# Rounding to fp8 once per tile in place of once per half: the VectorE queue of two attention passes

## What is computed

```python
def _div_clamp_fp8(x, scale):
    y = jnp.clip(x.astype(jnp.float32) / scale, -FP8_MAX, FP8_MAX)   # FP8_MAX = 448
    y = y.astype(jnp.bfloat16).astype(jnp.float32)
    return y.astype(jnp.float8_e4m3fn).astype(jnp.float32)

core = _gqa(q, k, v).reshape(b, s, nh * d)        # own keys and values
xout = _gqa(qx, kx, vx).reshape(b, s, nh * d)     # keys and values of the context
cat = jnp.concatenate([core, xout], axis=-1)
catq = _div_clamp_fp8(cat, proj_smooth)
return jnp.einsum('bsi,oi->bso', catq, wproj) * (proj_in_scale * proj_w_scale)
```

## Time and profile before

| | |
|---|---|
| time, median of 3 runs (lowest to highest) | 634.34 us (633.56 to 635.05) |
| the profiled execution: span from first to last instruction | 632.0 us |
| PE busy | 576.7 us, 91% |
| VectorE busy | 494.6 us, 78%, 924 instructions |
| ScalarE busy | 369.1 us, 58% |
| GpSimd busy | 365.9 us, 58% |
| mean granted TensorE clock | 0.986 |

### The profile page before, as it was taken

How to read it: one execution, slowest core, us unless ns; L and a number is a source line. 1 busy time by engine, 2 the same in 40 slices (tenths; PEclk the granted TensorE clock), 3 DMA queues, 4 the chain that set the end, 5 groups by cost and what they waited for, 6 DMA issues and landing times.

```text
span 632.0 us, 10614 instructions
## 1 busy us (share of the span) xinstructions
PE 576.7 (91%) x3735; PEld 468.2 (74%) x3738; DVE 494.6 (78%) x924; ACT 369.1 (58%) x669; POOL 365.9 (58%) x299
## 2 busy tenths in 40 slices
PE   3999679959869999999988999999999999999996
PEld 1664225635548888988977889888889888888886
DVE  4697999775999998999998889999997956333333
ACT  1559657757766776776766676667665235434221
POOL 4101495014578787868659967676777634855431
PEclk9999999988989999999998999999999999999999
DMA  7892113015512131031192141222210100310001
GB/s 219 272 348 77 60 50 117 34 67 152 180 33 106 35 111 58 1 134 35 48 357 96 37 124 57 86 84 85 59 43 18 35 0 3 117 37 30 1 2 67
DMA packets 44564, 54.87 MB, mean 87 GB/s; under 512 B 8416, under 2 KB 30816, under 8 KB 44512
## 3 DMA queue, kind: packets, MB, share of 16 engines
q1 hardware_dynamic: 44512, 54.20, 26.5%
HBM read 41.60 MB, written 12.58 MB: 86 GB/s over the span
## 4 chain that ended last, share of the span: by engine, by line
PE 64%; DVE 6%; POOL 3%; issue 3%; ACT 2%; DVEq 0%; POOLq 0%; ACTq 0%
PE g_proj L2217 13%; PE g_proj L2303 8%; PE g_scores L2258 7%; PE g_turn L2247 6%; PE g_op L2284 5%; PE g_op L474 3%; PE g_op L475 2%; PE g_op L476 2%; PE g_proj L459 2%; PE g_proj L461 2%; PE g_proj L460 2%; PE g_turn L2267 2%; PE g_op L2225 1%; POOL g_rs L1615 1%; PE g_turn L459 1%
## 5 line engine op out<-in xcount | busy, mean ns | idle before, releaser
L1615 POOL TENSOR_TENSOR g_rs<-g_ve,neg_half 128x4 f32<-128x4 f32 x80 | 83.7, 1052 | 36.4 <-DVE g_ve L1727 36.0
L1636 POOL TENSOR_TENSOR g_cat<-g_yb,g_kb 128x1024 fp32r<-128x1024 bf16 x32 | 70.9, 2224 | 41.3 <-DVE g_yb L1782 41.3
L2217 PE MATMUL g_proj<-w_hi,g_xqc 128*128 128x512 f32 x192 | 84.4, 439 | 6.7 <-ACT g_qn L2005 4.1
L2217 PE MATMUL g_proj<-w_lo,g_xqc 128*128 128x512 f32 x192 | 76.2, 397 | 0.0
L503 POOL TENSOR_TENSOR m_h_lo<-m_h,m_h_hi 128x512 fp32r<-128x512 f32 x32 | 41.4, 1297 | 57.1 <-ACT m_h_hi L490 57.1
L1727 DVE TENSOR_REDUCE g_ve<-g_sq 128x4 f32<-128x516 f32 x80 | 54.8, 685 | 16.9 <-ACT g_sq L1979 14.9
L2258 PEld LDWEIGHTS g_scores<-g_qkT 128*128 128x128 f32 x512 | 60.9, 192 | 2.7 <-issue 1.4
L2258 PE MATMUL g_scores<-g_qkT 128*128 128x64 f32 x512 | 61.0, 272 | 0.0
L2247 PE MATMUL g_turn<-ident,g_qn 128*128 128x128 f32 x384 | 58.2, 278 | 1.8 <-DVE g_qn L1740 1.5
L1979 ACT ACTIVATE g_sq<-g_proj 128x512 f32<-128x512 f32 x80 | 47.8, 597 | 16.7 <-PE g_proj L2217 15.2
L2247 PEld LDWEIGHTS g_turn<-ident,g_qn 128*128 128x128 f32 x384 | 44.8, 143 | 11.7 <-DVE g_qn L1740 3.6
(11 more groups left out here) (242 smaller groups left out, 1662.2 us busy)
## 6 DMA issues: line engine op xcount, KB each, us to landing
kvx_rows<-f_kept SPq DMA_DIRECT2D x24, 256.0 KB, 2.4
g_ksq<-kvx_rows SPq DMA_DIRECT2D x8, 512.0 KB, 4.5
g_kraw<-kvx_rows SPq DMA_DIRECT2D x16, 256.0 KB, 3.2
g_v<-kvx_rows SPq DMA_DIRECT2D x8, 512.0 KB, 4.2
m_raw<-in_L_W SPq DMA_DIRECT2D x16, 256.0 KB, 3.0
c_raw<-in_L_wqT SPq DMA_DIRECT2D x4, 512.0 KB, 6.2
f_w_ctx<-in_L_wkvxT SPq DMA_DIRECT2D x4, 512.0 KB, 8.0
c_praw<-in_L_wprojT SPq DMA_DIRECT2D x4, 512.0 KB, 5.6
```

Of the source, the lines that this page charges most:

```text
L1615: G.tensor_tensor(rs[:, at % NORMS, :], ve[:, at % NORMS, :], k["half"][:, 0:4], ALU.pow).then_inc(q["rs_done"], 1)
L1636: G.tensor_tensor(cat[:, h].rearrange("p h (b s) -> p b h s", b=2), yb[:, h, :].rearrange("p (b h s) -> p b h s", b=2, s=SEQ), kb[:, h, :] ...
L2217: last = T.matmul(bank(n, i)[:], xqc[:, n % 2, view * KT + c_, :], w[:, c_, :], start=c_ == 0 and part == 0, stop=c_ == KT - 1 and part == 1)
```

## The change

For tiles 0 to 14 the clip, the mask and the max-and-multiply run once over both halves (`powers(n)`, instructions of 128 by 2048), behind `unload(n, 1)` and `scale(m, 5)`; both `lift`s follow. `unload` and `lift` stay one per half, as do POOL's `fp8` and PE's `output_half`. In `both_cross` `lift(n, 0)` thereby moves from ahead of `scale(m, 4)` to the end of the step. The last tile keeps its two halves, in the same order as before. The semaphores `clipped`, `abs_done` and `k_done` count once per tile in place of twice. The queues of PE, ScalarE, POOL and SP are the same.

```diff
-                def clip(n, h):
-                    dve.wait_ge(q["q1_done"], n * 2 + h + 1)
-                    V.tensor_scalar(yb[:, h, :], yb[:, h, :], FP8_MAX, -FP8_MAX, ALU.min, ALU.max).then_inc(q["clipped"], 1)
-
-                def power(n, h):
-                    dve.wait_ge(q["clipped"], n * 2 + h + 1)
-                    V.tensor_scalar(kb[:, h, :].bitcast(U16), yb[:, h, :].bitcast(U16), 0x7F80, None, ALU.bitwise_and).then_inc(q["abs_done"], 1)
-                    dve.wait_ge(q["abs_done"], n * 2 + h + 1)
-                    V.tensor_scalar(kb[:, h, :], kb[:, h, :], FP8_NORMAL, FP8_LIFT, ALU.max, ALU.mult).then_inc(q["k_done"], 1)
+                def powers(n, halves=slice(0, 2)):
+                    y, power, done = yb[:, halves, :], kb[:, halves, :], (n + halves.stop if n == LAST else n + 1)
+                    dve.wait_ge(q["q1_done"], n * 2 + halves.stop)
+                    V.tensor_scalar(y, y, FP8_MAX, -FP8_MAX, ALU.min, ALU.max).then_inc(q["clipped"], 1)
+                    dve.wait_ge(q["clipped"], done)
+                    V.tensor_scalar(power.bitcast(U16), y.bitcast(U16), 0x7F80, None, ALU.bitwise_and).then_inc(q["abs_done"], 1)
+                    dve.wait_ge(q["abs_done"], done)
+                    V.tensor_scalar(power, power, FP8_NORMAL, FP8_LIFT, ALU.max, ALU.mult).then_inc(q["k_done"], 1)
 
                 def lift(n, h):
-                    dve.wait_ge(q["k_done"], n * 2 + h + 1)
+                    dve.wait_ge(q["k_done"], n + h + 1 if n == LAST else n + 1)
...
                     unload(n, 0)
-                    clip(n, 0)
-                    power(n, 0)
                     scale(m, 4)
                     sums(m, 5)
                     unload(n, 1)
-                    clip(n, 1)
                     scale(m, 5)
-                    power(n, 1)
+                    powers(n)
                     lift(n, 0)
                     lift(n, 1)
...
                     unload(n, 0)
-                    clip(n, 0)
                     sums(m, 5)
-                    power(n, 0)
-                    lift(n, 0)
                     scale(m, 4)
                     unload(n, 1)
                     scale(m, 5)
-                    clip(n, 1)
-                    power(n, 1)
+                    powers(n)
+                    lift(n, 0)
                     lift(n, 1)
```

More of the change, by code:

```diff
@@ L1915, in _ @@
                     both_cross(n)
[L1916 to L1920, removed]
                 less_max(LAST, 0)
@@ L1932, in _ @@
                 unload(LAST, 0)
-                clip(LAST, 0)
-                power(LAST, 0)
+                powers(LAST, slice(0, 1))
                 lift(LAST, 0)
@@ L1937, in _ @@
                 moe.hidden(dve, 0, 1)
-                clip(LAST, 1)
-                power(LAST, 1)
+                powers(LAST, slice(1, 2))
                 lift(LAST, 1)
```

## The result

The changed kernel takes 654.4 us (median of 4 runs, 653.9 to 656.9) against 634.2 us (633.6 to 635.1) in the same session: 1.0322 times as long, with a 95% interval of 1.0291 to 1.0352, so 20.3 us more. The prediction was 652.8 us.

What follows compares the result with a forecast made beforehand. PE's chain was taken to bound the kernel, VectorE's saving counting nothing; cross pass 13.3 plus own pass 5.2 us gave 18.5 on a 632.0 us span, 650.5, plus 2.3 for the median: 652.8 us, range 646 to 658.

Steps and rivals of the forecast that it cites:

- What holds the end: Both passes: PE's chain sets the pace, so VectorE's saving of 0.55 us per tile, 8.3 us in all, gains nothing.
- own pass: First pass: POOL 0.93 us later at everything that follows; 2.8 + 0.9 + 1.5 = 5.2 us lost.
- A: Moment in each tile: the end of attend(n, 1), from which on VectorE has the second half.
- The cross tiles 8 to 13: PE waits ahead of output_half: 2.16 us behind tiles 8 and 9 (4.3), 1.58 behind 10 to 13 (6.3).
- the choice between 2.52 and 2.14: Cross pass: duration of fp8(n, 0) in us; 2.52 taken, as beside lift(1); 2.14 kept for the range, 2.7 us less.
- Tile 7: Cross pass, where POOL also splits output weights and has no gap: later fp8(n, 1) costs 2.7 us.
- rival (c): PE's clock falls with every wait; behind seven cross waits 9.5 us more, 662.3 us; chance 0.05.
- own steps 2, 4 and 6: Own pass: ScalarE's key-chunk scaling waits for the first rstd; 0.43 of 0.93 us covered, 0.50 each, 1.5 in sum.
- The upper bound of the range: High end 656.9 us: 0.4 more at turn_p seven times (+2.8), 0.93 in steps 2, 4, 6 (+1.3); range to 658.
- Own steps 1, 3 and 5: Own pass: POOL's queue behind fp8 has no room; PE's idle time ahead of turn_p grows 0.93 us each, 2.8.
- VectorE's busy time: Sign in the changed kernel's profile: some 8 us less busy time on VectorE, its idle time grown by more.
- the clock was not 1.00 behind tile 7: Sign in the cross pass: PE's clock stays at 1.00 behind the new waits of 1.5 to 2.2 us in seven tiles.

Runs made afterwards that it cites:

- Late POOL: Kernel before, with one idle POOL power of 128x4 behind fp8(n, 1) in steps n = 0 to 5: 639.8 us, 1.0087.
- its control: The changed kernel again, same instructions and order, with semaphores that count in another way: 655.3 us, 1.0327.
- the cross pass alone: Kernel before, with the changed order and merged instructions in the cross pass (tiles 7 to 14) only: 649.0 us, 1.0232.
- the clip left out: Kernel before, without the clip of half 0 in tiles 0 to 14: 634.4 us, 1.0005.
- late VectorE: Kernel before, with one idle VectorE instruction of some 0.8 us behind lift(n, 1) in own steps n = 0 to 5: 638.6 us, 1.0063.
- tiles 8 to 14 alone: Kernel before, with the changed order and merged instructions in tiles 8 to 14 only: 645.6 us, 1.0184.
- the early step left out: Kernel with only the cross pass changed, less late_tokens(3) in tile 7: 646.4 us, 1.0194, from two runs.
- the kernel with 1.08 us waits in each own step: Changed kernel with clip, mask and max-and-multiply at the same place but once per half, unmerged: 664.3 us, 1.0482 against the kernel before.

## Why the prediction was right, and where it wasn't

**What holds the end.** Held. The chain is PE's, and VectorE's saving ends in a wait for PE ahead of `unload(1)`. The reading behind it held for the own pass only, where `unload(1)` waited for PE before, too: in the cross pass it came 0.68 us behind A by VectorE's own queue, so "waits for PE's A either way" came true only with the change. The sum loses nothing by it, for it has `unload(1)` start at A + 0.08. On the price of the instructions the Trainium skill (VectorE: DVE Perf Modes, section "The TRN2 errata") is borne out: 0.69 us for one of 2048 against two of 0.42 to 0.43, and at an equal place merging was worth 0.33 us a tile. But what an instruction costs its engine and what its place costs the next engine are two sums.

**The cross tiles 8 to 13.** Held: the start of `fp8(n, 0)` at A + 4.73 (4.77 forecast), its pair 4.60 us long (4.65), the waits 2.29, 2.24 and 1.38 to 1.43 us (2.16 and 1.58), the cost 2.2, 2.05 and four times 1.6 (2.16 and 1.58). `fp8` beside `lift(1)` took 2.51, so the choice between 2.52 and 2.14 went the way of the earlier trace rows. `turn_p` took nothing more.

**Tile 7.** The mechanism held, the size was short: 3.5 us for 2.7. Without the fall of the clock it was 2.5. Of the seven cross waits this is the one behind which rival (c) came true.

**The term that was short: own steps 2, 4 and 6.** The prediction followed POOL alone there, found 0.43 us of cover ahead of ScalarE's scaling, and put 0.50 on each. For POOL this is near: with the cover of a quarter of a microsecond and ScalarE 0.92 us later in the changed kernel, the step would have lost some 0.65 by POOL alone (an estimate from these two). What it overlooked is VectorE's own queue: behind the lifts stands `less_max` of the next tile, `scores(n, 1)` waits for it, and that path has no cover in even steps. So each lost 0.93 to 0.96, the whole of the delay, 1.3 us more in the sum; own pass 6.5 for 5.2. The rule that every instruction queued behind a delayed one has a waiter was kept for POOL and not for the engine that was changed. The upper bound of the range had this 1.3 us, for another reason.

**Own steps 1, 3 and 5.** Here the cost held, 0.9 us each, and its place didn't. PE's wait ahead of `turn_p` did not grow, it stayed at 0.28 to 0.30, and 0.75 stood ahead of `scores(n, 1)`. Late POOL alone would have cost as much (0.96 of 1.01), so the term came out right by another path than its own. Two other signs failed: VectorE's busy time fell by 4.8 us and not by some 8, and the clock was not 1.00 behind tile 7.

**The sum.** 18.5 us forecast; by the trace 21.7 without the late start, 3.2 more: 1.3 for the even steps, 0.8 behind tile 7, 0.7 for the first half-clock stretch of the cross pass, 0.4 behind the loops. The medians differ by only 20.3 because the profiled execution is the longest of its four, by 2.3 to 3.0 us; 1.46 of these are the late start, for the rest there is no trace. So it is in part luck that 652.8 lies so near to 654.4.

## What to carry to other kernels

Before merging two instructions of a pipeline into one, find the consumer of the first half: it now waits for the second half and for the whole width, and that wait, not the saved fixed cost, decides when another engine sets the pace. When an instruction moves within a queue, list the waiter of every instruction behind it on the same engine as well as on the next one. An experiment that moves without merging, and one that shortens without moving, separate the two effects in two runs.

## What the runs showed of the hardware

**The clock's answer to a wait is not fixed by its length.** The prediction read from one row that the clock stays at 1.00 behind 2.90 us of idle time. The same wait of 2.90 us, before anything that the change touches, stands in all 13 traces. Behind it the clock was 0.50 in seven (the changed kernel, its control, the cross pass alone, the clip left out, late VectorE, tiles 8 to 14 alone, the early step left out) and 1.00 in six. Of the changed kernel's trace:

```profile
88.00:90.00 2.00, 2.00 (x4) 1.01 (x3) 2.00 (x3) 1.19 (x3) 2.00 (x2) 0.50 0.32 122
```

Behind a wait of 1.94 us 20 us earlier it fell in three of 13. Behind 2.24 to 2.57 us it fell at tile 7 in four traces, with a longer wait and a half-clock stretch some 10 us ahead, and not in the one without these; behind tiles 8 and 9 it never fell at waits of 2.2 to 2.6. In the kernel with 1.08 us waits in each own step it fell behind three of six. What decides between these was not settled. The spread of the runs goes with it: spans of one kernel from 637.9 to 642.2 us at mean clocks of 0.983 to 0.976.

**Whoever starts first holds the other up.** `lift` (VectorE, two inputs in SBUF) and `fp8` (POOL) never ran beside each other undisturbed. Where `lift(1)` started first it took its usual time and `fp8` 2.51 us; where `fp8` started first it took 2.14 and `lift(1)` 2.25, against 0.69 alone. The exclusive lock of the Trainium skill (SBUF — State Buffer, section "SBUF: two separate sides") agrees with both. In the second case VectorE is the one that stands still, until the POOL instruction is done: `lift(1)` ended at 437.59, 0.55 us behind the end of `fp8`. It holds for the smallest instructions too: POOL's idle power of 128x4 took 1.00 to 1.01 us in three steps, and 1.45 in the three where VectorE's two products of L202, with two SBUF inputs each, had begun 0.3 us before it.
